# Causal mask added by the VectorE instruction that finds the row extreme of the scores, in PSUM, in place of a bf16 matmul per query block

## What is computed

```python
q = _rope(jnp.einsum('btm,mhd->bthd', x, w_aq))
k = _rope(jnp.einsum('btm,mhd->bthd', x, w_ak))
v = jnp.einsum('btm,mhd->bthd', x, w_av)
s = jnp.einsum('bihd,bjhd->bhij', q, k) / D_HEAD
s = s - jnp.asarray(INF_APPROX, x.dtype) * mask        # mask is 1 where i < j, INF_APPROX 1e30
p = jax.nn.softmax(s, axis=-1)
o = jnp.einsum('bhij,bjhd->bihd', p, v)
```

## Time and profile before

| what | value |
|---|---|
| median of 3 runs | 1098.11 us (1096.88 to 1100.96) |
| span of the profiled execution | 1099.5 us |
| own time of the profiled execution beside its span | not listed apart from the three runs; the span stands 1.4 us above their median |
| busy share of the span | PE 92%, LDWEIGHTS 76%, DVE 81%, ACT 60%, POOL 54% |
| scores of the first block, of the last | 29.7 us, 794 us |
| idle time of PE before the first scores | 12.8 us, until the low part of q and k is there |

### The profile page before, as it was taken

The page is one execution under the profiler, slowest core; times in us unless marked ns, Lnnn a source line. Parts: engine busy times, 40 slices in busy tenths (PEclk is TensorE's granted clock), DMA queues, the critical chain, the costliest instruction groups (busy, mean ns, idle before and its releaser), DMA issues. The chain is left out here.

```text
span 1099.5 us, 20887 instructions
## 1 busy us (share of the span) xinstructions
PE 1008.7 (92%) x5648; PEld 837.4 (76%) x5648; DVE 890.4 (81%) x1803; ACT 657.7 (60%) x1383; POOL 598.5 (54%) x536
## 2 busy tenths in 40 slices
PE   2699999999999999999999999999939999999995
PEld 1588787877878787887878788788727878788784
DVE  4888898989988899998889999898855758576744
ACT  4476776767776676777767777676625252252531
POOL 3667767777777778777777877777540100000000
PEclk8799999999999999999999999999978999999998
DMA  8542222732223242222223122222020000000000
GB/s 281 164 134 49 58 72 63 218 86 57 57 50 74 58 114 86 57 57 61 64 67 105 48 57 58 67 64 60 1 78 1 1 1 20 1 19 0 1 20 19
DMA packets 33838, 69.99 MB, mean 64 GB/s; under 512 B 5520, under 2 KB 7056, under 8 KB 32272
## 3 DMA queue, kind: packets, MB, share of 16 engines
q1 hardware_dynamic: 30976, 62.81, 21.4%
q10 hardware_dynamic: 2832, 6.82, 1.7%
HBM read 24.26 MB, written 7.34 MB: 29 GB/s over the span
## 5 line engine op out<-in xcount | busy, mean ns | idle before, releaser
L737 POOL TENSOR_SCALAR probs<-probs,inv_sum 128x128 f32<-128x128 f32 (+7 forms) x256 | 237.6, 928 | 178.5 <-DVE inv_sum L653 178.5
L554 ACT ACTIVATE pT<-psum 128x512 fp32r<-128x512 f32 (+3 forms) x384 | 176.7, 490 | 146.9 <-PE psum L420 144.7
L310 PE MATMUL psum<-pT,vals 128*128 128x512 f32 (+3 forms) x1152 | 246.9, 355 | 1.6 <-DVE rT L695 1.6
L542 ACT ACTIVATE probs<-psum,neg_max 128x128 f32<-128x128 f32 (+7 forms) x256 | 190.5, 744 | 52.5 <-DVE neg_max L647 49.0
L663 DVE TENSOR_TENSOR pT<-psum,pT 128x512 fp32r<-128x512 f32 (+3 forms) x384 | 199.8, 547 | 15.7 <-ACT pT L554 12.6
L310 PEld LDWEIGHTS psum<-pT,vals 128*128 128x128 f32 x1152 | 191.8, 193 | 24.1 <-DVE pT L663 1.7
L647 DVE TENSOR_REDUCE neg_max<-psum 128x1 f32<-128x128 f32 (+7 forms) x256 | 190.9, 746 | 11.0 <-PE psum L411 10.9
L420 PE MATMUL psum<-ident,probs 128*128 128x128 f32 x1152 | 178.5, 281 | 21.9 <-DVE pT L663 15.4
L742 POOL TENSOR_TENSOR swapped<-swapped,rope 128x512 f32<-128x512 f32 x128 | 165.4, 1292 | 40.5 <-DMA swapped<-proj 40.4
L749 POOL TENSOR_TENSOR qk<-swapped,qk 128x512 fp32r<-128x512 f32 x128 | 179.4, 1402 | 3.6 <-ACT qk L574 3.6
L918 PE MATMUL ps<-hid,w 128*128 128x512 f32 x768 | 181.3, 396 | 0.0
(11 more groups left out here) (78 smaller groups left out, 1241.7 us busy)
## 6 DMA issues: line engine op xcount, KB each, us to landing
swapped<-proj SPq DMA_DIRECT2D x256, 128.0 KB, 2.3
w_stage<-qk_split SPq DMA_DIRECT2D x30, 256.0 KB, 2.7
x_static<-x_moving SPq DMA_DIRECT2D x4, 1024.0 KB, 5.0
wv_stage<-v_split SPq DMA_DIRECT2D x15, 256.0 KB, 2.6
x_split<-ffn_raw ACTq DMA_DIRECT2D x2, 1024.0 KB, 5.9
ffn_raw<-g SPq DMA_DIRECT2D x2, 1024.0 KB, 8.0
x_moving<-x_split SPq DMA_DIRECT2D x2, 1024.0 KB, 4.9
out<-y SPq DMA_DIRECT2D x4, 512.0 KB, 2.6
```

The costliest lines, as they stand in the source:

```text
L310: ins = nc.tensor.matmul(out_ap, left[a], right[b], start=first and i == 0, stop=last and i == 2)
L542: nc.scalar.activation(probs[:, ib % 4, :width].rearrange("p (h c) -> p h c", h=halves), score_ps[:, ib % 2, :halves, :half], ACT.Exp, bia ...
L554: nc.scalar.activation(pT[chunk][:, 0, 4 * f:4 * f + n_blocks, (ib % 4) * P:(ib % 4 + 1) * P], bank("t", head[1], nth)[:, :n_blocks * P].r ...
L737: nc.gpsimd.tensor_scalar(p, p, inv_sum[:, n:n + 1], 1.0, ALU.mult, ALU.mult).then_inc(probs_ready[0], 1)
```

## The change

The mask matmul and its two bf16 operands go. DVE's reduction becomes one `tensor_tensor_reduce`: it reads the scores from PSUM and a row of mask values from SBUF, adds them, writes the sum back to the same place in PSUM, and keeps the row's extreme. As the fused operation that is used has no negated output, the scores are computed with the opposite sign (`SCORE_SCALE` is -1/D), the mask value becomes +1e30, the extreme is a minimum, and the exponential is taken with scale -1. The mask is now a bf16 tile of 128 x 1024, zero but for its last 128 columns, and block `ib` reads its last (ib + 1) x 128 columns. It is loaded as fp32 (512 KB in place of 64 KB) and cast by one DVE instruction in place of two. A semaphore increment of its own (`max_passed`) stands ahead of the fused instruction on DVE.

```diff
-SCORE_SCALE = 1.0 / D
-MASKED = -1e30
+SCORE_SCALE = -1.0 / D
+MASKED = 1e30
+MIN_START = 3e38
...
-    ident_b = sb("ident_b", [P, P], BF16)
-    mask_b = sb("mask_b", [P, P], BF16)
+    mask = sb("mask", [P, T], BF16)
...
-    mask_f = sb("mask_f", [P, P], F32, pre)
+    mask_f = sb("mask_f", [P, T], F32, pre)
...
                     nc.tensor.matmul(dst, left[0], right[0], start=True, stop=False)
-                    if h == halves - 1:
-                        nc.tensor.matmul(dst[:, half - P:], ident_b[:], mask_b[:], start=False, stop=False)
                     nc.tensor.matmul(dst, left[0], right[1], start=False, stop=False)
...
-                    pe.wait_ge(masks_ready, 1)
+                    pe.wait_ge(consts_loaded, 48)
...
-                                     score_ps[:, ib % 2, :halves, :half], ACT.Exp,
+                                     score_ps[:, ib % 2, :halves, :half], ACT.Exp, scale=-1.0,
...
+                if is_first(head) and ib == 0:
+                    dve.wait_ge(mask_ready, 1)
                 wait_for(dve, scores_ready, head, ib)
+                dve.sem_inc(max_passed, 1)
                 halves, half = score_halves(ib)
-                nc.vector.tensor_reduce(neg_max[:, n:n + 1], score_ps[:, ib % 2, :halves, :half], AX.XY, ALU.max,
-                                        negate=True).then_inc(max_ready[0], 1)
+                minus_scores = score_ps[:, ib % 2, :halves, :half]
+                row_mask = mask[:, T - (ib + 1) * P:].rearrange("p (h c) -> p h c", h=halves)
+                nc.vector.tensor_tensor_reduce(minus_scores, minus_scores, row_mask, 1.0, MIN_START, ALU.add, ALU.min,
+                                               neg_max[:, n:n + 1]).then_inc(max_ready[0], 1)
...
-                    nc.vector.tensor_copy(ident_b[:], ident[:])
-                    nc.vector.tensor_copy(mask_b[:], mask_f[:]).then_inc(masks_ready, 1)
+                    nc.vector.tensor_copy(mask[:], mask_f[:]).then_inc(mask_ready, 1)
```

More of the change, by code:

```diff
@@ L169, in attention @@
     w_saved, x_saved, warm_zero = sem("w_saved"), sem("x_saved"), sem("warm_zero")
-    r_zero, masks_ready = sem("r_zero"), sem("masks_ready")
+    r_zero, mask_ready = sem("r_zero"), sem("mask_ready")
     W_SAVED, X_SAVED = 16 * (len(weight_parts) + 2), 16 * (B - 2)
@@ L197, in attention @@
     x_moved = sem("x_moved")
-    pool_passed = sem("pool_passed")
+    pool_passed, max_passed = sem("pool_passed"), sem("max_passed")
     def score_halves(ib):
@@ L596, in step @@
                     act.wait_ge(x_low, B)
-                    act.wait_ge(masks_ready, 1)
+                    act.wait_ge(mask_ready, 1)
                 if is_first(head) and s == NI - 1:
@@ L1204 @@
         "ident_in": np.eye(P, dtype=np.float32),
-        "mask_in": np.triu(np.full((P, P), MASKED, np.float32), 1),
+        "mask_in": np.concatenate([np.zeros((P, T - P), np.float32), np.triu(np.full((P, P), MASKED, np.float32), 1)], axis=1),
         "f1": c(by_tile(take("ffn_w1_w"), 1)),
```

## The result

The changed kernel takes 1103.45 us (1101.02 to 1105.52), the kernel before 1097.62 on the same chip. The medians are 5.8 us apart. The ratio, which goes by all the runs and not by the two medians alone, is 1.0046, with a 95% interval of 1.0028 to 1.0064: clear of noise, just inside the 0.5% that counts as equal here, and on the other side of the forecast of 1087. Matmuls that the prediction priced at 31 us are gone, and nothing came of it.

The account below looks back on a forecast made before the run. PE was taken to set the pace before, DVE after: 21.6 + 0.64 + 0.55 + 0.7 = 23.5 us a head for 23.9, 13 us gained. 1099.5 - 13 + 1.6 = 1088.3 profiled, 1087 as median; range 1072 to 1119.

Parts of the forecast that it names:

- The bound: Steady attention: PE sets the pace before, DVE is longer after; a head takes 23.5 us in place of 23.9.
- PE's gain: PE in attention: each removed mask matmul saves about 0.12 us, 0.96 a head, 31 us if PE stays the bound.
- over 0.8: Sign in steady attention: PE's waits for pT grow from 0.4 us a head to more than 0.8.
- DVE's price: DVE's fused pass in attention: PSUM write and extreme's read-out add 0.08 us a block, 0.64 a head.
- DVE's price is the upper one: Rival, DVE's fused pass: drain wait or PSUM write costs, say, 0.2 us a block, 1117 us; chance 0.22.
- The fused pass runs at half the rate: Rival, DVE's fused pass: another 0.51 us per 512 columns, 147 us in all, about 1235; chance 0.06.
- DVE is the bound already: Rival, attention: all DVE's added 20 us count and nothing comes back, 1120 us; chance 0.06.
- The rotary wait: DVE's wait at the rotary sum in step 2: falls from 1.27 to about 0.55 us a head.
- The start: Before the first scores: mask load grows from 64 to 512 KB, costing 1.6 us.
- It cancels: Rival, attention: price near 0.13 us a block or idle time doesn't shrink, 23.9 a head, 1094 to 1103; chance 0.18.
- Wrong in kind if both engines have more idle time: Sign, PE and DVE: the prediction fails in kind if both idle more than before; no size given.

Follow-up runs that it names:

- e14: Kernel before without the mask matmul of blocks 3 to 7, those diagonal blocks left unmasked: 1100.94 us, ratio 1.0031.
- e13: Kernel before without the mask matmul of blocks 0, 1 and 2, those diagonal blocks left unmasked: 1098.16 us, ratio 1.0003.
- e1b: Kernel before with every mask matmul taken out and nothing added on DVE, diagonal blocks left unmasked: 1102.24 us, ratio 1.0032.
- e5b: Kernel before with DVE's cosine product reading the projection from its PSUM bank, held until then, not the SBUF copy: 1081.33 us, ratio 0.9848.
- e3b: Changed kernel with the 64 KB mask load of before, the zero columns set by a DVE memset: 1099.52 us, ratio 1.0012 to the kernel before.
- e2b: Changed kernel with the mask matmul put back, so the mask is added twice: 1101.31 us, ratio 1.0023 to the kernel before.
- e4b: Changed kernel with four overwritten 512-column matmuls a head just ahead of block 7's scores: 1097.76 us, ratio 0.9991 to the kernel before.
- e7b: Kernel before with two overwritten 512-column matmuls a head ahead of block 7's scores: 1091.56 us, ratio 0.9943.
- e15: Kernel before without any mask matmul, with four overwritten 512-column matmuls a head ahead of block 7's scores: 1094.90 us, ratio 0.9975.

## Why the prediction was wrong

- **The bound (the step that failed).** I took a head's length as the work of the longer engine plus what idle time would be left to it: "21.6 + 0.64 + 0.55 + 0.7 = 23.5". No engine is the longer one. A pair is as long as the circle of three legs, and the sum should have asked of each removed matmul on which leg it stands. Five of eight stand where PE waits for DVE at the end (e14: nothing gained), three where they count, and in part (e13: 0.22 us a pair, 3.5 us in all). The forecast gained 13. The rows for it were on the table: PE waits for `pT` 25 times, as often as there are heads, which said that PE's time ahead of that wait is free.
- **PE's gain.** The 0.12 us a block was right, by the starts in both profiles (0.70 and 0.58 us for the scores of block 2), though the 0.62 us in its working is three times 0.21: the unmasked group there took 0.67 (434.33 to 435.00). PE's busy time fell by 13.8 us in 25 heads, 0.55 a head and not about 1, since rows overlap. Its waits for `pT` grew to 0.88 us a head, as forecast ("over 0.8"), but for the wrong reason: DVE was not late, PE was early, as e1b shows.
- **DVE's price.** 0.08 us a block was taken, 0.01 measured start to start. The write into PSUM and the mask stream together with the read-out come to no more than that. With 0.01 the forecast's own arithmetic gives 21.6 + 0.08 + 0.78 + 0.7 = 23.2 us a head (0.78 being what then stays of the rotary wait, by the same path) and about 1076, farther from the result: a better number in a wrong frame. The rivals "DVE's price is the upper one" and "The fused pass runs at half the rate" fall with it, and with DVE's 700 ns.
- **DVE is the bound already.** It falls as well: DVE's occupancy is 91% in the steady part, and 0.01 us a block is all that was added. But the rule of the Trainium skill that I had set beside it (Perfetto Trace Analysis, Identifying the Most-Contended Engine) named the engine where time was to be had, and on that the runs agree: the time that e5b takes off DVE's product and, with it, POOL's gave 9 us by the pairs, while e1b's matmuls, 31 us by the forecast's price, gave 3.7. Occupancy alone did not tell which part of an engine's work counts.
- **The rotary wait** was to fall from 1.27 to 0.55 us; it fell to 1.06 and 1.09. It is what the circle leaves over, and not a store of idle time.
- **The start.** 1.6 us forecast, 1.04 between the first scores of before and after, and 1.6 between those of e3b and after. Right in kind and near in size.
- **It cancels** gave 1094 to 1103 and comes nearest in time. Its words, "two engines this close to full wait for each other in turn", were half the truth; the gain of 0.23 and the loss of 0.2 us a pair cancel (e1b, e2b), and the start adds 1.0. The lower end of its time was 1094, but the measured 1103.45 lies beyond its upper end, by what the clock took.
- **The clock** was in no rival. I read 0.99 over 600 us as full speed and did not ask what made up the hundredth. With the pairs unchanged and 1.0 us from the start, it is what is left for the other 4.8 us; that it has this size is worked out as the remainder, and that removing PE's work lowers it is seen in the runs' clocks (0.963, and 0.961 in e1b).
- "Wrong in kind if both engines have more idle time" did not come about in full: PE's grew, DVE's fell from 57.7 to 52.9 us of 600.

## What to carry to other kernels

Where two engines are near full and wait for each other once a round, follow one round of the waits from event to event and add up its legs; work is worth something only on the leg that it stands on, and a wait beside it is where a saving will go. Then look at what the freed engine does with its idle time: here TensorE was granted 1.2 GHz more often, so compare pairs without such a stretch, and the granted clock of the runs, before blaming the new instruction. A two-operand VectorE instruction that could take one operand from PSUM is worth a try beside a busy GpSimd.

## What the hardware showed that I had not expected

- A read-out of an accumulator on DVE is a row of 139 ns, but the instruction behind it starts at the same time for blocks of 384 columns and more (443.91 and 443.91), and 0.09 to 0.10 us later for those of 128 and 256 (446.49 to 446.59). There too it starts no later behind the pass than it did behind the reduction.
- Two to four useless matmuls of 512 columns a head made the kernel 6 to 7 us faster (e4b, e7b, e15), with the pairs without a stretch at 1.2 GHz unchanged and a higher mean granted clock (0.979 in place of 0.971 on e7b's chip).
- What GpSimd does beside it can make up a third of a VectorE row: 991 to 683 ns in the mean for DVE's product, once it has one SBUF operand, while POOL's went from 1401 to 1287. With both operands in SBUF it took 0.68 us in the median of the 27 rows with POOL idle beside them, and 1.05 to 1.18 in the 62 rows with POOL busy for most of them (the kernel before, 100 to 700 us).
